# Two rotary projections: fp32 products against three fp32r passes with the rotation reading PSUM

## What is computed

```python
x = x + L0_xattn(layernorm(x), ctx)      # 16 heads of 16, keys and values from ctx
x = x + L0_attn(layernorm(x))            # self attention over the 16 batches, rotated
x = x + L0_ffn(layernorm(x))             # 8 experts, top 2, capacity
x = x + L1_xattn(layernorm(x), ctx)      # as L0_xattn, with an additive key bias
x = x + L1_attn(layernorm(x))            # self attention over the 64 positions, rotated
x = x + L1_ffn(layernorm(x))             # fp4-quantised gated network
# in both self attentions:
q, k, v = x @ Wq + bq, x @ Wk + bk, x @ Wv + bv      # biases in L0 only
q, k = rope(q), rope(k)                              # t * cos + swapped(t) * sin
```

## Time and profile before

| | us |
|---|---|
| median of 3 runs | 1368.52 |
| lowest, highest | 1367.79, 1369.06 |
| profiled execution, its own time | 1370.81 |
| span of the profiled execution (first to last instruction) | 1369.0 |
| mean granted TensorE clock in it, as a share of full speed | 0.935 |

### The profile page before, as it was taken

The page is one execution under the profiler, slowest core; times in us unless marked ns, Lnnn a source line. Parts: engine busy times, 40 slices in busy tenths (PEclk is TensorE's granted clock), DMA queues, the critical chain, the costliest instruction groups (busy, mean ns, idle before and its releaser), DMA issues. The chain is left out here.

```text
span 1369.0 us, 35013 instructions
## 1 busy us (share of the span) xinstructions
PE 1233.9 (90%) x12294; PEld 1036.5 (76%) x12294; DVE 972.0 (71%) x1995; ACT 784.7 (57%) x1435; POOL 634.9 (46%) x580
## 2 busy tenths in 40 slices
PE   5999999999999689539998999999999999777778
PEld 4788888888888458429985788888888888546455
DVE  5777777777777576456526877777777777578896
ACT  3677777777776211115444677777777776224221
POOL 3666656656664214032332656566656654325000
PEclk9999999999999885559999999999999999887999
DMA  7786776776765120434537776776776765100000
GB/s 223 208 212 177 184 203 175 185 202 178 190 166 139 45 55 2 152 132 152 198 131 223 198 202 177 191 195 176 179 207 175 189 168 135 37 0 3 1 8 24
DMA packets 106725, 198.33 MB, mean 145 GB/s; under 512 B 43661, under 2 KB 63790, under 8 KB 106640
## 3 DMA queue, kind: packets, MB, share of 16 engines
q1 hardware_dynamic: 105104, 193.32, 52.8%
q0 software_dynamic: 1536, 3.88, 0.8%
HBM read 88.26 MB, written 10.62 MB: 72 GB/s over the span
## 5 line engine op out<-in xcount | busy, mean ns | idle before, releaser
L913 POOL TENSOR_SCALAR cross_prob<-cross_prob,cross_inverse 128x1024 f32<-128x1024 f32 x256 | 287.7, 1124 | 327.5 <-DVE cross_inverse L647 327.5
L844 ACT ACTIVATE cross_prob<-cross_negated,cross_negmax 128x1024 f32<-128x1024 f32 x256 | 295.0, 1152 | 135.7 <-DVE cross_negmax L639 135.4
L639 DVE CUSTOM_DVE_ANT_0 cross_negated<-cross_scores,cross_bias 128x1024 f32<-128x1024 f32 x256 | 313.6, 1225 | 25.7 <-PE cross_scores L513 8.1
L526 PEld LDWEIGHTS cross_turn<-ident,cross_prob 128*128 128x128 f32 x2048 | 237.9, 140 | 47.3 <-POOL cross_prob L913 9.7
L526 PE MATMUL cross_turn<-ident,cross_prob 128*128 128x128 f32 x2048 | 268.0, 273 | 6.3 <-POOL cross_prob L913 4.6
L853 ACT COPY cross_probT<-cross_turn 128x512 f32<-128x512 f32 x256 | 149.4, 584 | 63.6 <-PE cross_turn L526 62.7
L655 DVE COPY cross_probT<-cross_turn 128x512 f32<-128x512 f32 x256 | 175.5, 686 | 0.0
L513 PE MATMUL cross_scores<-cross_keys,cross_qbd 96*128 96x512 f32 x512 | 169.5, 412 | 2.8 <-POOL cross_qbd L905 2.8
L893 POOL TENSOR_TENSOR cross_ctx_lo<-cross_raw,cross_ctx_hi 128x512 fp32r<-128x512 f32 x120 | 154.7, 1291 | 14.1 <-DVE cross_probT L715 8.3
L456 PE MATMUL cross_out<-cross_wv_hi,cross_ctx_lo 128*128 128x256 f32 x488 | 147.4, 302 | 0.0
L458 PE MATMUL cross_out<-cross_wv_hi,cross_ctx_hi 128*128 128x256 f32 x488 | 137.3, 281 | 0.0
(11 more groups left out here) (283 smaller groups left out, 2120.3 us busy)
## 6 DMA issues: line engine op xcount, KB each, us to landing
cross_keys<-cross_key_hi SPq DMA_DIRECT2D x512, 128.0 KB, 2.4
cross_raw<-in_ctxT SPq DMA_DIRECT2D x32, 1024.0 KB, 5.6
cross_keys<-cross_key_lo SPq DMA_DIRECT2D x256, 128.0 KB, 2.4
cross_bias<-bias_rows SPq DMA_DIRECT2D x32, 512.0 KB, 3.7
up_sb<-in_moe_w SPq DMA_DIRECT2D x8, 1024.0 KB, 9.3
down_sb<-in_moe_w SPq DMA_DIRECT2D x8, 1024.0 KB, 5.7
cross_stacked_q<-q_rows SPq DMA_DIRECT2D x90, 64.0 KB, 2.0
q_rows<-cross_negated SPq DMA_DIRECT2D x8, 256.0 KB, 2.3
```

What stands on the lines that cost most here:

```text
L526: last = pe.transpose(ps_t[part][:, k * P:(k + 1) * P], prob[n % 2][:, kt * P:(kt + 1) * P], ident)
L639: dve.tensor_tensor_reduce(negated[n % 2], ps_s[n % 2][:, :], bias_sb[par][:, :], -1.0, 3.0e38, ALU.add, ALU.min, negmax[:, n % 2:n % 2 + ...
L844: act.activation(prob[n % 2][:, :], negated[n % 2], ACT.Exp, bias=negmax[:, n % 2:n % 2 + 1], scale=-1.0, accum_out=total[:, n % 2:n % 2 + ...
L913: pool.tensor_scalar(prob[n % 2][:, :], prob[n % 2][:, :], inverse[:, n % 2:n % 2 + 1], 1.0, ALU.mult, ALU.mult).then_inc(prob_ready, 1)
```

## The change

- The 256 x 768 weights are no longer loaded in the project block. In the next to last batch of the cross attention SP loads them to `raw`, which then holds no context any more (`load_behind`); for self0 a second DMA spreads the biases of q and k over 32 partitions beside them.
- In the last batch ScalarE rounds them in three pieces of 128 x 512 to `ctx_hi`, in steps 0, 1 and 2 (`round_behind`), and GpSimd takes the rest of each piece to `ctx_lo` in steps 2, 3 and 4 (`rest_of_behind`). For self0 the bias follows: ScalarE rounds it in step 3, and in step 5 GpSimd runs four instructions over 32 partitions x 512, which put the rounded bias in the even halves of the 32 partitions and the rest in the odd ones (`bias_parts`).
- In the normalize block ScalarE's copy is rounded to fp32r, and VectorE takes the rest of each of the four buffers out of PSUM (`divide`). TensorE may write a PSUM buffer again only when VectorE has done so.
- In the rope block each fp32 product becomes three fp32r passes; in self0 one more product over 32 partitions adds the bias of q and k. The copy of q and k out of PSUM is gone: the multiplications by cosine and sine read PSUM. q and k have a semaphore of their own, so that VectorE starts before v is made. The addition of v's bias moves to the end of VectorE's tile.
- The last stage takes the buffer `xn` of self1 in place of one of its own.

```diff
@@ normalize_block
+            def divide(j):
+                dve.wait_ge(copied, j + 1)
+                dve.tensor_tensor(in_order(xnT_lo, j), turned_by(j), in_order(xnT, j).bitcast(F32), ALU.subtract
+                                  ).then_inc(divided, 1)
...
             for i in range(NT):
                 dve.tensor_scalar(xn[:, i, :], x[:, i, :], moments[:, i, 0:1], rstd[:, i:i + 1],
                                   ALU.subtract, ALU.mult).then_inc(normed, 1)
+                if xnT_lo is not None and i in (5, 7):
+                    divide(i // 2 - 2)
+            if xnT_lo is not None:
+                divide(2)
+                divide(3)
...
-                    pe.wait_ge(copied, i // 2 - 1)
+                    pe.wait_ge(copied if xnT_lo is None else divided, i // 2 - 1)
@@ First
+    def load_behind(self, sp):
+        sp.dma_start(self.raw[:, :, 0:3 * D], self.w["behind"]).then_inc(self.behind_loaded, 16)
+        if "behind_bias" in self.w:
+            sp.dma_start(self.raw[0:2 * HD, :, 3 * D:], self.w["behind_bias"]).then_inc(self.behind_loaded, 16)
...
+    def rest_of_behind(self, pool, part, half_mask):
+        at = slice(part * D, (part + 1) * D)
+        if part < 3:
+            pool.wait_ge(self.behind_rounded, part + 1)
+            pool.tensor_tensor(self.ctx_lo[:, :, at], self.raw[:, :, at], self.ctx_hi[:, :, at].bitcast(F32), ALU.subtract
+                               ).then_inc(self.behind_divided, 1)
+        elif "behind_bias" in self.w:
+            bias, hi = (t[0:2 * HD, :, at] for t in (self.raw, self.ctx_hi))
+            pool.wait_ge(self.behind_rounded, part + 1)
+            pool.tensor_tensor(bias, bias, hi.bitcast(F32), ALU.subtract).then_inc(self.bias_step, 1)
+            pool.wait_ge(self.bias_step, 1)
+            pool.tensor_scalar(bias, bias, half_mask[0:2 * HD, 1:2], 1.0, ALU.mult, ALU.mult).then_inc(self.bias_step, 1)
+            pool.tensor_scalar(hi, hi.bitcast(F32), half_mask[0:2 * HD, 0:1], 1.0, ALU.mult, ALU.mult).then_inc(self.bias_step, 1)
+            pool.wait_ge(self.bias_step, 3)
+            pool.tensor_tensor(self.bias_parts, bias, hi.bitcast(F32), ALU.add).then_inc(self.bias_step, 1)
@@ cross_block, ScalarE and GpSimd
+                    if in_last(b, 1) and n < 4:
+                        if n == 0:
+                            act.wait_ge(value_ready, 4 * (B - 1))
+                        first.round_behind(act, n)
...
+                    if in_last(b, 1) and 2 <= n < 6:
+                        first.rest_of_behind(pool, n - 2, half_mask)
@@ rope_block
+            def project(out, i, cols, ends):
+                for k in range(G):
+                    x_hi, x_lo = (t[:, k, i * P:(i + 1) * P] for t in xnT)
+                    w_hi, w_lo = (t[:, k, cols] for t in (first.ctx_hi, first.ctx_lo))
+                    pe.matmul(out, x_lo, w_hi, start=(k == 0), stop=False)
+                    pe.matmul(out, x_hi, w_lo, start=False, stop=False)
+                    last = pe.matmul(out, x_hi, w_hi, start=False, stop=(ends and k == G - 1))
+                return last
...
-                    pe.wait_ge(qk_copied, i - 1)
+                    pe.wait_ge(rotated, 3 * (i - 1))
+                last = project(ps_qk[i % 2][:, :], i, slice(0, 2 * D), b_row is None)
+                if b_row is not None:
+                    if i == 0:
+                        pe.wait_ge(cleared, 1)
+                    last = pe.matmul(ps_qk[i % 2][:, :].rearrange("p (g d) -> p g d", g=2), ones[:, :],
+                                     first.bias_parts, start=False, stop=True)
+                last.then_inc(qk_projected, 1)
...
-                dve.wait_ge(projected, i + 1)
...
+                x = ps_qk[i % 2][:, :].rearrange("p (c h d) -> p c h d", c=2, h=H)
+                dve.wait_ge(qk_projected, i + 1)
```

More of the change, by code:

```diff
@@ L434, in body @@
             def body(b, par):
+                if in_last(b, 2) and not in_last(b, 1):
+                    sp.wait_ge(lo_done, 4 * B)
+                    first.load_behind(sp)
                 if not in_last(b, 1):
@@ L996, in rope_block @@
         sem = lambda n: ctx.enter_context(nc.semaphore(f"{tag}_{n}"))
-        qk = [sb(f"qk{i}", [P, 2, H, HD]) for i in range(2)]
         straight, swapped = sb("straight", [P, 2, H, HD]), sb("swapped", [P, 2, H, HD])
@@ L1837, in __init__, with gated_block @@
             ("stats", [6]), ("rstd", []), ("shifted", []), ("half_power", [])))
-def gated_block(nc, tag, aT, ahead, gate_upT, downT, ident, out):
+def gated_block(nc, tag, aT, ahead, xn, gate_upT, downT, ident, out):
     with ExitStack() as ctx:
@@ L2181, in attend @@
                 if n == 1:
-                    gated_block(nc, "gated", oT, ahead, gate_upT, downT, eye, out)
+                    gated_block(nc, "gated", oT, ahead, xn, gate_upT, downT, eye, out)
                 scope.pop()
```

80 lines of the change are left out of this document (44 added, 36 removed).

## The result

| | before | changed |
|---|---|---|
| median, us | 1369.08 (15 runs) | 1377.50 (15 runs) |
| lowest, highest | 1367.45, 1376.27 | 1371.04, 1381.23 |
| ratio, 95% interval | | 1.0051 (1.0038 to 1.0065) |
| profiled execution, its own time and span | 1370.81, 1369.0 | 1376.31, 1374.5 |

A forecast was written before the change was run, and what follows sets the result against it. TensorE and VectorE were both taken as full in the rope blocks, TensorE setting the pace. -5.4 - 4.5 + 3.0 + 2.05 + 2 x 0.64 + 2.15 = -1.4 us, from 1368.5 to 1367.1; range 1363.5 to 1371.5.

The forecast's parts named there:

- Self1: Second self attention: rope block 24.9 us against 30.3, -5.4; normalize block +2.05, with subtractions of 0.69.
- Self0's normalize block: Ahead of self0's rope block: strided subtractions of 0.98 us each make it +3.0, bounds 1.95 and 3.6.
- Self0's rope block: First self attention: TensorE alone sets the pace, 26.8 us against 31.3, -4.5.
- or, with the bias product of the same 512 columns, 1.71: Self0's rope block: q and k of a tile fall from 1.72 to 1.71 us, bias product included.
- the first 3.6 us run at half clock as before: Start of both rope blocks: half clock for 3.6 us, costing 1.8 us in each.
- The rounding in step 0: Last batch of each cross attention: ScalarE's rounding delays what waits behind it, +0.64 each.
- three subtractions: GpSimd in cross1's last batch: three of 1.27 us fit, the division of step 6 on time, 0.
- +2.15 was forecast: Cross0's last batch: GpSimd's four bias instructions, 3.85 us, delay the last turns, +2.15, bounds 0 and 2.4.
- The rival of the clock: Slower, 1372.5 us, 15%: half clock after TensorE's wait in cross0 and for longer in both rope blocks.
- its first two places: Cross0's last batch, then self0's rope block: a 3.6 us stretch at half clock in each, giving away 1.8.
- Once tiles run, TensorE is no idler than now: Argument about the rope blocks against the rival of the clock, which was given 15%.
- The other rivals: Cheap additions 1363.9, 20%; passes at a quarter 1363.1, 5%; VectorE bounding self1 1368.0, 10%; rope blocks otherwise bound 1372, 5%.

The follow-up runs named there:

- e6: Changed kernel with the bias over 128 partitions and GpSimd's four bias instructions behind step 7 of cross0's last batch: 1365.86 us, ratio 0.9965.
- e5: Changed kernel with GpSimd's four bias instructions, still 32 partitions, behind the addition of step 7 in cross0's last batch: 1372.26 us, ratio 1.0019.
- e15: The changed kernel measured once more, no edit: 1377.99 us, ratio 1.0066 to the kernel before.
- e3: Changed kernel with the bias of q and k over 128 partitions in place of 32: 1370.48 us, ratio 1.0015.
- e1: Only self1 and the last batch ahead of it changed, self0 and cross0 as in the kernel before: 1367.49 us, ratio 0.9983.
- e2: Changed kernel without the bias of q and k in self0, its product and GpSimd instructions left out: 1366.21 us, ratio 0.9974.
- e16: e6 measured again, no edit: 1365.71 us, ratio 0.9977.
- e18: e1 measured again, no edit: 1367.82 us, ratio 0.9979.
- e9: e6 with an unread product of 32 partitions x 512 columns added to every tile of self1's rope block: 1371.62 us, ratio 0.9995.

## Why the prediction was wrong

By its own steps, changed kernel against before, from the two profiles:

- **Self1, right.** Forecast -5.4 for the rope block and +2.05 for the normalize block. From the first product to the last copy it takes 23.98 us (1204.16 to 1228.14), against 30.3: -6.3; the normalize block 8.95 against 7.09: +1.9. The tile is 2.55 us, not 2.64, since the turn takes 0.36 of it and not 0.45.
- **Self0's normalize block, right.** +3.0 forecast, +2.8 measured, with the subtraction at 1.01.
- **Self0's rope block, wrong, and the largest miss.** Forecast 26.8 us, measured 32.8 (484.91 to 517.73), +1.5 in place of -4.5. The step that failed is "or, with the bias product of the same 512 columns, 1.71": a duration read from 128-row passes was given to a product of 32 rows. It takes 0.63 us out of the tile and not 0.23, by the tile 0.43 more than a 128-row product, 3.4 us in all. No row showed 32 rows between 128-row passes, and unlike GpSimd's instructions this operation got no bounds. The second part is "the first 3.6 us run at half clock as before": it was 12.5 us, 8.0 more than in e6, which at 0.43 is 3.5 us. With 128 rows and an early rise the block takes 28.54 - 2.4 = 26.1 us (e6), near the forecast 26.8, so the rest of the step held; 26.1 + 3.4 + 3.5 is 33.0, against 32.8 measured.
- **Cross0's last batch, right up to the last division, and low behind it.** The rounding in step 0 was to cost 0.64 in each cross attention. From the division of step 1 to that of step 2 it is 4.16 us (438.82 to 442.98) against 3.82 before (435.91 to 439.73), and as much in e6 and in cross1: +0.34. From step 2 to step 6 cross1, e5 and e6 take 11.88 us as before, as was forecast for three subtractions; with the bias in step 5 it is 14.91, and the last division follows after 1.79 in place of 2.69: +2.13, where +2.15 was forecast. What had no term is the stretch behind the last division, up to the normalize block: 14.46 us (459.68 to 474.14) in place of 11.89 (454.30 to 466.19), +2.6. In it the clock is at 0.50 for 3.4 us. The same stretch takes 13.3 us in e15, where the clock falls too, and 12.8 in e3, where it doesn't; without the gap 11.9 to 12.8 (e1, e2, e5, e6, e16, e18). So a part of the 2.6 is scatter.
- **The rival of the clock** had 15%, and its first two places came true: the clock falls behind the gap in cross0 (the last turn of 1.81 us), and it stays down longer in self0's rope block. But the gap doesn't always bring the fall: it does in the changed kernel and in e15, and in e3 the clock stays at 1.00 through a gap of 2.85 us and the turns behind it. And the link between the two places was wrong. The late rise doesn't hang on the gap or the fall in cross0: e5 and e9 have neither ahead of their late rises (13.0 and 12.7). "Once tiles run, TensorE is no idler than now" was true and no protection. In self1, which has no 32-row product, nothing of it happened. So the warning about the clock was luck in self0's rope block: the place was right, the cause was not.
- **The other rivals fell.** 32 partitions on GpSimd cost what 128 do; fp32r passes took 0.233; VectorE didn't bound self1.

In sum, from the two profiles: the forecast of -1.4, +6.0 for self0's rope block (26.8 against 32.8), +2.6 behind cross0's last division, and -0.3 each for the rounding in cross0 and cross1, -0.2 each for the two normalize blocks and -0.9 for self1's rope block. That gives +5.3, and the two profiled executions are 5.5 apart. That the medians are 8.4 apart is where the two profiled executions lie among the others, as said with the result.

## What to carry to other kernels

A matmul is priced by its shape, not its columns alone: in this kernel one small product with fewer rows between full ones also delayed the passes around it, 0.63 us in place of 0.23, so it is worth padding to full rows where the operand is cheap to widen. Work put on an idle engine has to be placed by who waits behind it and who shares its port; here the same four instructions cost 2.1 us in one place, and up to 2.6 more behind it, 1.9 in another and nothing that shows in a third. And where a block begins at half clock, unused products in TensorE's waits ahead of it can be worth as much as the rewriting of a block (3.0 and 3.5 us here, for both layers together, against 1 to 2 for all of self0's change without its flaws).

## What the runs showed of the hardware that was not expected

- A rope block with TensorE busy throughout stayed at half clock for 12.4 to 13.0 us in four of seven starts with 32-row products (7.7, 8.0 and 3.7 in the others), and at most 6.2 in 24 without. The Trainium skill (TensorE: Matmul & The Clock Gate, section The HAM clock gate) says that sustained activity lifts the clock and that the moment varies from run to run; the 24 agree, the four go beyond it.
- VectorE's normalisations took 2.3 times as long beside GpSimd's instructions (4.64 against 2.03 us for six).
- GpSimd took 1.27 and 0.68 us for 32 partitions and 1.30 and 0.69 for 128.
- After a wait of TensorE of 2.8 us the clock fell in two profiles (changed kernel, e15) and stayed at 1.00 in a third with the same wait (e3).
